# The first stage of a graph-attention kernel in another order: scores from PSUM, adj's first pair in two contiguous blocks masked on GpSimd, chunk steps between sides

## The reference

```python
h = maximum(layernorm(x), 0)                     # 4096 x 128
h = h @ W.T + b_W
e = (h @ a1)[:, None] + (h @ a2)[None, :] + b_a[0]
e = where(e > 0, e, 0.2 * e)                     # 4096 x 4096
scores = where(adj > 0, e, -9e15)
out = x + softmax(scores, axis=1) @ h
```

## Time and profile before

| | |
|---|---|
| median of 3 runs | 202.6 us (202.4 to 202.87) |
| span of the profiled execution | 200.8 us; its own time outside the span isn't recorded, the median is 1.8 us above it |
| TensorE busy | 194.9 us, 97% |
| VectorE | 183.0 us, 91% |
| ScalarE | 147.9 us, 74% |
| GpSimd | 52.4 us, 26% |
| DMA | 75.66 MB, 377 GB/s over the span |
| granted TensorE clock | 1.00 (2.4 GHz) throughout |

### The profile page before, as it was taken

How to read it: one execution, slowest core, us unless ns; L and a number is a source line. 1 busy time by engine, 2 the same in 40 slices (tenths; PEclk the granted TensorE clock), 3 DMA queues, 4 the chain that set the end, 5 groups by cost and what they waited for, 6 DMA issues and landing times.

```text
span 200.8 us, 7230 instructions
## 1 busy us (share of the span) xinstructions
PE 194.9 (97%) x3183; PEld 189.2 (94%) x3183; DVE 183.0 (91%) x265; ACT 147.9 (74%) x192; POOL 52.4 (26%) x66
## 2 busy tenths in 40 slices
PE   7969999999999999999999999999999999999993
PEld 7648889999999999999999999999999999999993
DVE  4779999999998799897999999999999999999745
ACT  2679879898882777689988888899588888996000
POOL 1002479699995010205000000072000000510000
PEclk9999999999999999999999999999999999999999
DMA  5999999999999999999999999999999999997012
GB/s 181 376 417 418 407 403 423 421 418 415 422 432 408 418 423 419 416 421 418 415 419 423 419 418 421 421 411 421 419 418 418 415 421 416 418 383 226 6 43 66
DMA packets 15968, 75.66 MB, mean 377 GB/s; under 512 B 1600, under 2 KB 5952, under 8 KB 7616
## 3 DMA queue, kind: packets, MB, share of 16 engines
q1 hardware_dynamic: 15792, 75.06, 91.7%
q10 hardware_dynamic: 144, 0.13, 0.3%
HBM read 73.08 MB, written 2.11 MB: 374 GB/s over the span
## 4 chain that ended last, share of the span: by engine, by line
PE 91%; DMA 4%; SPq 1%; DVE 1%; issue 1%; POOL 0%
PE ps L836 29%; PE ps L834 29%; PE ps L840 29%; DMA adj_sb<-in_adj_t 4%; PE ps L808 2%; PE ps L798 2%; SPq L268 1%; SPq L273 1%; PE ps L876 1%; DVE mask L476 0%; POOL bad L788 0%; DVE rden L504 0%; DVE rg L510 0%; DVE bad L519 0%; DVE upper L576 0%
## 5 line engine op out<-in xcount | busy, mean ns | idle before, releaser
L834 PE MATMUL ps<-V,w 128*128 128x129 f16 x1024 | 174.3, 221 | 0.0
L836 PE MATMUL ps<-V,w 128*128 128x129 f16 x1024 | 174.3, 221 | 0.0
L840 PE MATMUL ps<-V,w 128*128 128x129 f16 x1024 | 174.3, 221 | 0.0
L379 ACT ACTIVATE mask<-adj_sb 128x1024 bf16<-128x1024 int32 x126 | 125.5, 1056 | 28.6 <-DMA adj_sb<-in_adj_t 28.6
L459 DVE SCALAR_TENSOR_TENSOR w<-g_row,pairs,mask 128x1024 f32<-128x1024 f32 x96 | 120.5, 1320 | 5.5 <-ACT mask L379 3.6
L834 PEld LDWEIGHTS ps<-V,w 128*128 128x128 f16 x1024 | 100.2, 98 | 1.5 <-ACT H L340 0.7
L836 PEld LDWEIGHTS ps<-V,w 128*128 128x128 f16 x1024 | 100.2, 98 | 1.0 <-issue 1.0
L840 PEld LDWEIGHTS ps<-V,w 128*128 128x128 f16 x1024 | 100.2, 98 | 0.0
L459 DVE SCALAR_TENSOR_TENSOR w<-ps,pairs,mask 128x1024 f32<-128x1024 f32 x31 | 37.4, 1267 | 0.0
L785 POOL TENSOR_TENSOR xT<-xT,x_sb 128x512 f32<-128x512 f32 x6 | 11.5, 1932 | 79.8 <-ACT xT L394 79.8
L739 POOL TENSOR_TENSOR x_sb<-x_sb,b_row 128x512 f32<-128x512 f32 x8 | 10.0, 1301 | 0.0
(11 more groups left out here) (93 smaller groups left out, 63.8 us busy)
## 6 DMA issues: line engine op xcount, KB each, us to landing
adj_sb<-in_adj_t SPq DMA_DIRECT2D x64, 1024.0 KB, 10.3
xT<-in_x_t SPq DMA_DIRECT2D x8, 256.0 KB, 7.5
x_sb<-in_x_p SPq DMA_DIRECT2D x3, 512.0 KB, 10.9
g_row<-g_dram SPq DMA_DIRECT2D x1, 1536.0 KB, 10.3
out<-xT SPq DMA_DIRECT2D x3, 512.0 KB, 9.9
x_sb<-in_x_p SPq DMA_DIRECT2D x2, 256.0 KB, 4.2
out<-xT SPq DMA_DIRECT2D x1, 192.0 KB, 3.4
out<-xT SPq DMA_DIRECT2D x3, 64.0 KB, 1.6
```

Source lines behind the costliest of these rows:

```text
L379: nc.scalar.activation(mask[:, m % MASKS, r], adj_sb[:, m % HELD, r], ACT.Relu, scale=CONNECTED).then_inc(mask_ready, 1)
L834: nc.tensor.matmul(sums[:, bank, a, :], w16[:, m % SLOTS, col:col + P, 1], V[:, jt, 0, 0:NF], start=(jt == 0 and a == 0), stop=False, skip ...
L836: nc.tensor.matmul(sums[:, bank, a, :], w16[:, m % SLOTS, col:col + P, 1], V[:, jt, 1, 0:NF], start=False, stop=False, skip_group_check=True)
L840: last = nc.tensor.matmul(sums[:, bank, a, :], w16[:, m % SLOTS, col:col + P, 0], V[:, jt, 0, 0:NF], start=False, stop=(jt == NT - 1), ski ...
```

## The change

Scores of the first part are multiplied out of PSUM, by a new `first_scores` on VectorE as soon as the projections of chunks 0 and 1 are there; ScalarE copies these chunks to H only after that. The first pair of adj lies in DRAM as two contiguous blocks, one for each side, and is loaded by two transfers, the first of them ahead of x's chunks 2 and 3. Both of its masks are made by GpSimd. The low parts of chunk 0 and all of chunk 1 also go to GpSimd. The bias load is issued behind the load of m = 9. On TensorE `h_chunk(2)` comes behind the spread, the first pair's products with the low parts come last within its first side, and projection and centring steps stand between the sides of pairs 1 and 2. On ScalarE the masks of pairs 2 to 4 come later among the chunk steps. On GpSimd the deviations of the last sets come ahead of chunk 3's V.

```diff
-    H_BANK = (1, 4, 1, 4, 4, 4, 4, 4)
+    H_BANK = (1, 4, 4, 4, 4, 4, 4, 4)
+    V_AT = (1, 1, 2, 3, 4, 4, 5, 6, 7, 7, 8, 8, 9, 9)
...
@@ SP: loads
+                halves = adj_t[0, :, :].rearrange("p n -> (p n)").rearrange("(s p n) -> s p n", s=2, p=P)
                 load_xt(0)
+                load_x(0)
                 load_xt(1)
-                load_x(0)
                 load_x(1)
+                sp.dma_start(adj_sb[:, 0, 0:GC], halves[0, :, :]).then_inc(adj_begun, 16)
                 load_xt(2)
+                load_xt(3)
+                sp.dma_start(adj_sb[:, 0, GC:2 * GC], halves[1, :, :]).then_inc(adj_loaded[0], 16)
                 load_x(2)
-                load_xt(3)
-                load_adj(0)
+                load_adj(1)
                 load_xt(4)
-                load_adj(1)
...
                     load_adj(m)
+                    if m == BIAS_AT:
+                        sp.dma_start(b_row[:], b_W.rearrange("(a n) -> a n", a=1).to_broadcast([P, DOUT])
+                                     ).then_inc(b_row_loaded, 16)
@@ ACT
                 def take_chunk(c):
                     act.wait_ge(h_done, c + 1)
+                    if c < 2:
+                        act.wait_ge(scores_ready, 1)
...
                 roots_part()
+                nc.scalar.activation(warm[:], zero_col[:], ACT.Exp)
                 take_chunk(0)
+                weights(0)
                 take_chunk(1)
-                nc.scalar.activation(warm[:], zero_col[:], ACT.Exp)
                 relu_chunk(2)
-                weights(0)
+                highs(0)
                 relu_chunk(3)
-                highs(0)
-                first_mask()
                 take_chunk(2)
                 mask_part(1)
                 take_chunk(3)
                 relu_chunk(4)
-                highs(1)
-                mask_part(2)
                 take_chunk(4)
                 relu_chunk(5)
+                mask_part(2)
+                take_chunk(5)
+                relu_chunk(6)
                 weights(1)
                 mask_part(3)
-                take_chunk(5)
-                relu_chunk(6)
-                mask_part(4)
                 take_chunk(6)
                 relu_chunk(7)
+                mask_part(4)
+                take_chunk(7)
                 mask_part(5)
-                take_chunk(7)
@@ DVE
+                def first_scores():
+                    dve.wait_ge(h_done, 2)
+                    dve.wait_ge(std_ready, 2)
+                    for c in range(2):
+                        r = slice(c * CT, (c + 1) * CT)
+                        of = ps[:, H_BANK[c]:H_BANK[c] + 2, 0:2 * (2 + DOUT)].rearrange("p k (a n) -> p k a n", a=2)
+                        by = rstd[:, 1, r].rearrange("p (k a n) -> p k a n", k=2, n=1).to_broadcast([P, 2, 2, 2])
+                        ins = nc.vector.tensor_tensor(st[:, r, :].rearrange("p (k a) n -> p k a n", k=2),
+                                                      of[:, :, :, 0:2], by, ALU.mult)
+                    ins.then_inc(scores_ready, 1)
...
+                (statistics(1), norm, 1/std, first_scores, maximum of the scores,)
                 (then the three instructions on cc and the two on gg, then the read-back and the shifts)
-                early_mask()
+                step_(nc.vector.tensor_scalar(rstd[:, 2, 0:GI], rstd[:, 1, 0:GI], gg[:, 1:2], None, ALU.mult))
+                inverse_scales(0)
                 pack(0)
                 scale_weights(0)
-                products(0)
                 weigh_first(0)
-                lows(0)
                 weigh_first(1)
                 weigh(0, 1)
-                statistics(2, 5, 8)
+                statistics(2)
                 weigh(1, 0)
                 weigh(1, 1)
-                products(1)
-                lows(1)
+                statistics(3)
+                weigh(2, 0)
                 scores(1)
-                weigh(2, 0)
                 weigh(2, 1)
                 pack(1)
                 scale_weights(1)
-                statistics(3)
                 weigh(3, 0)
+                statistics(4)
                 weigh(3, 1)
-                statistics(4)
@@ GpSimd
+                def first_mask(side):
+                    if side == 0:
+                        pool.wait_ge(adj_begun, 16)
+                    else:
+                        pool.wait_ge(adj_loaded[0], 16)
+                    r = slice(side * GC, (side + 1) * GC)
+                    nc.gpsimd.tensor_scalar(mask[:, 0, r], adj_sb[:, 0, r], CONNECTED, 0.0, ALU.mult,
+                                            ALU.max).then_inc(mask_early if side == 0 else mask_first, 1)
+                first_mask(0)
+                first_mask(1)
+                first_lows()
+                halves(1)
                 deviations(2, 3)
-                halves(2)
+                halves(2, 0, 2)
+                halves(2, 2, 4)
+                deviations(3, 5)
                 halves(3)
-                deviations(3, 5)
@@ PE
+                centre_chunk(0), wa, norm, centre_chunk(1), h_chunk(0), h_chunk(1), cc
                 (transpose of the maxima, centre_chunk(2), centre_chunk(3), spread)
+                h_chunk(2)
+                first_pair()
                 h_chunk(3)
                 centre_chunk(4)
-                whole(0)
+                side_products(1, 0, 0, GI)
                 h_chunk(4)
                 centre_chunk(5)
-                whole(1)
+                side_products(1, 1, 0, GI).then_inc(mm_done, 1)
                 h_chunk(5)
                 centre_chunk(6)
-                whole(2)
+                side_products(2, 0, 0, GI)
                 h_chunk(6)
                 centre_chunk(7)
-                whole(3)
+                side_products(2, 1, 0, GI).then_inc(mm_done, 1)
                 h_chunk(7)
-                for m in range(4, NM - ENDS):
+                for m in range(3, NM - ENDS):
```

157 lines of the change are left out of this document (77 added, 80 removed).

## The result

The change makes the kernel slower: 208.27 us median (207.81 to 210.54) against 202.5 in the runs beside it, a ratio of 1.0296 with a 95% interval of 1.0238 to 1.0354. The profiled execution has a span of 206.7 us where the kernel before had 200.8. The forecast was 203.2, range 201.7 to 204.3: wrong in size by 5 us and outside its range.

The account below looks back on a forecast made before the run. TensorE's fixed sequence of attention products was taken as the bound. To 202.6 us were added 0 for the start, 0.45 for chunk 3's late V and 0.2 for the eighth pair: 203.2, range 201.7 to 204.3 (own range 202.4 to 204.5).

Parts of the forecast that it names:

- What bounds the kernel: TensorE's attention products are fixed work, 2.72 us a pair; only the sequence's start and holes in it change the time.
- Part 1, the chain to the pack: Projections, scores, maximum and exponentials before the first pack: pack ready at 11.55, 1.8 us earlier if nothing stands in its way.
- Part 2, the mask's price: First pair's masks on GpSimd: 1.2 us each, range 0.95 to 2.1, the second lying from about 11.5 to 12.7.
- Part 3, what the mask does to the pack: GpSimd's second mask holds VectorE's first pack until it ends: spread at 13.37, 1.0 of the 1.8 us lost.
- Rival (a): First pack on VectorE not held by the second mask: faster, 202.05 us, or 201.5 without the later hole; chance 0.28.
- Part 4, behind the spread: Chunk 2's projection, 0.89 us, now behind the spread, cancels the 0.79 gained: put at 0, no hole for low parts.
- Part 5: Sides, chunk steps, work taken from VectorE and the moved bias load: 0.
- Parts 6 and 7: TensorE waits 0.45 us at the seventh pair for chunk 3's V from GpSimd, then 0.2 for the eighth pair's weighting.
- rival (c): Holes at the seventh and eighth pairs don't open, since GpSimd starts chunk 3's V earlier: 202.5 us; chance 0.12.
- (b): Mask on GpSimd takes 2.5 us or more: 204.5 us, or 206.5 at 3.5 us a mask; slower, chance 0.10.

Follow-up runs that it names:

- e9_fewer_fillers: Changed kernel with 34 calls of float32 products that nobody reads, put on TensorE ahead of its wait for the first low parts; 214.43 us.
- e12_changed_again: The changed kernel once more, unaltered, on the same chip as a run with 17 filler calls; 209.42 us.
- e4_price: Kernel before, with six mask-like instructions of various types and sizes on GpSimd ahead of its deviations, results unused; 218.25 us, a time that means nothing.
- e7_masks_on_vector: Changed kernel with both first-pair masks on VectorE and ScalarE's order for the second pair as before; 202.52 us, 1.0003 of the kernel before.
- e10_v3_first: Changed kernel with chunk 3's V put back ahead of the last sets' deviations on GpSimd; 210.95 us.

## Why the prediction was wrong, step by step

- *What bounds the kernel*: right. The sequence of products is fixed work, and the loss is a late point of it plus holes in it; behind the eighth pair nothing changes.
- *Part 1, the chain to the pack*: the order was right, its start was not. The scores are done at 10.11 and the maximum is read back at 11.00, not 9.4 and 10.25; the pack starts at 12.26, 1.09 earlier than before and not 1.8. The term that failed is the end of the projections, 9.83 and not 9.05: the first two centring products, from 4.79 to 6.50, go at half the pace of the next two (0.86). The tables print a granted clock of 1.00 there, but the trace has no record of the clock before 6.51, and the pace tells the level: in every trace products go at half the pace until the records begin and at the full one from there, as between the levels of 1.2 and 2.4 GHz. In e9_fewer_fillers the warm-up products are 0.21 us apart up to its first record at 4.12 and 0.11 behind it; the two centring products take 0.87 there. In the kernel before the full pace begins at 4.83, in the other runs between 4.12 and 10.22, whatever the order. So the walk was right for a full pace from the start (in e9_fewer_fillers the projections end at 8.65 and the pack begins at 11.10), and when the pace rises is a term that the forecast didn't have. The 0.8 us for the five moved small instructions was right (10.22 to 11.00).
- *Part 2, the mask's price*: this is the step that failed. "It is nearer to the fill, and I take 1.2, with 0.95 to 2.1 for the range": it takes 3.645. Neither row was of such an instruction; a fill reads nothing, and a two-input multiplication, taken for the upper bound because it reads more, is the faster of the two. The halves landed at 8.26 and 10.84, 0.7 earlier than reckoned, which gave nothing, since GpSimd didn't start before 10.16. That start is a second miss in the same step: the trace of the kernel before has fills from 0.5 us on and arithmetic from 18.8 on, so no row showed when arithmetic can begin. No run divides the hole between the two. By the rows, masks of 1.2 us would have been through at 12.6 even from 10.16 on, and masks of 3.6 us begun at the landing would have ended at 15.6, 1.9 earlier than they did: as an estimate the price is enough for nearly the whole hole, and the start is worth up to half of it.
- *Part 3, what the mask does to the pack*: failed as well, since the hold has another length than the mask. VectorE's timeline of the kernel after, first and third pack, then GpSimd's masks and one instruction of VectorE in e9_fewer_fillers and in e12_changed_again:

```profile
12.26 0.18 DVE L583 TENSOR_SCALAR bounded<-eg 128x16 f32<-128x16 f32 x1 [0.24 <-ACT eg L367]
12.47 0.17 DVE L586 TENSOR_SCALAR upper<-bounded 128x16 int32<-128x16 int32 x1
12.68 0.18 DVE L589 CAST pairs<-upper 128x16 f16<-128x16 f32 x1
...
13.93 1.41 DVE L472 SCALAR_TENSOR_TENSOR w<-ps,pairs,mask 128x512 f32<-128x512 f32 x2 [0.93 <-POOL mask L763]
...
45.78 0.61 DVE L586 TENSOR_SCALAR upper<-bounded 128x32 int32<-128x32 int32 x1
46.43 0.55 DVE L589 CAST pairs<-upper 128x32 f16<-128x32 f32 x1
```

```profile
11.21 7.28 POOL L763 TENSOR_SCALAR mask<-adj_sb 128x1024 bf16<-128x1024 int32 x2 [9.78 <-DVE H L567]
11.31 0.98 DVE L586 TENSOR_SCALAR upper<-bounded 128x16 int32<-128x16 int32 x1
```

```profile
11.18 7.28 POOL L763 TENSOR_SCALAR mask<-adj_sb 128x1024 bf16<-128x1024 int32 x2 [9.75 <-issue]
11.58 0.68 DVE L639 TENSOR_SCALAR rstd<-rstd,gg 128x8 f32<-128x8 f32 x1
```

  In the profile of the change the first pack runs at its full pace in the middle of a 3.6 us mask that began 2.1 us before it; the third, beside a multiplication on GpSimd, is held to that instruction's end as in the earlier trace rows. But a mask does hold VectorE at its beginning. In the seven other traces with the first mask on GpSimd one tensor-by-constant instruction of VectorE takes 0.42 to 0.98 us instead of about 0.2, and each time it ends 1.06 to 1.08 us behind the mask's start (11.21 + 1.08 = 12.29 and 11.18 + 1.08 = 12.26 above), while the mask goes on for 2.6 us more; in e4_price it is 1.27 (the 0.59 at 14.87). In the profile of the change no instruction of this kind with more than one column began in that stretch, 10.16 to 11.24. The forecast had the second mask meet the pack, begun at 11.48 against 11.55; if the second mask holds as the first does, which no run shows, the pack's first instruction would have ended at 12.56 instead of 12.73, whatever the mask's price. In this run it was the first mask that lay beside the pack, and it had begun early enough. The rule of the Trainium skill that the prediction weighed (SBUF — State Buffer, Who interferes with whom), that the first to issue keeps the ports for its whole instruction, agrees with the third pack and not with the masks. Rival (a)'s condition, a pack that isn't held, was met in this run; its gain did not follow.
- *Part 4, behind the spread*: "net 0" is right, as e7_masks_on_vector shows by itself: spread 0.93 earlier, pair 4 at the same time. That the spread (13.08, in the range given of 13.0 to 13.7) and the first product (14.87 against 15.2) came out near the forecast is luck: the late scores took 0.7 of the 1.0 us that the hold of the pack was to take. "No hole" is wrong. The low parts were walked to 15.9 from free factors; that GpSimd must first be through with both masks entered the sum only as 1.2 us ending at 12.7. They came at 19.68. The prediction asked what the mask delays on VectorE, and not enough what is queued behind it on its own engine.
- *Part 5*: 0, right: from the spread to pair 4 e7_masks_on_vector takes 34.35 - 13.23 = 21.12 us, the kernel before 34.33 - 14.16 = 20.17, and of the 0.95 between them chunk 2's projection is 0.89; from pair 1 to pair 4 the changed kernel takes 14.56 and e7_masks_on_vector 14.53.
- *Parts 6 and 7*: right in mechanism and size: 0.54 and 0.14 against 0.45 and 0.2. The releasers are those named (GpSimd's subtraction for chunk 3), and in e10_v3_first the hole is gone with the deviations behind V. But they are one of two causes: e7_masks_on_vector keeps them ahead of V and has no such hole either. There ScalarE makes the second part's exponentials earlier, so GpSimd begins chunk 2's V 5.5 us behind pair 1 (25.33 - 19.82) and not 8.4 (33.37 - 25.00). That is rival (c)'s condition, brought about by another order. A slip of addition, 39.6 for 39.7 in TensorE's walk, makes the forecast of this hole 0.1 too long; another, 201.5 for 201.6 in rival (a), changes nothing.
- *The rivals*: (b) had the true engine, price and sign, with 0.10 and the sentence "No row speaks for such a price". For 3.5 us it gave 206.5. It let the masks start at 9.0 and so end at 16.0 instead of 17.44, took the late thing to be the pack, where it was the low parts two instructions further down GpSimd's queue, and left out the clock, 1.64.

The sum, forecast against measured: parts 1 to 4, 0 against a rest of -0.1 without the masks' queue; the hole, 0 against 3.7; the clock, 0 against 1.6, a term that the forecast didn't name; parts 6 and 7, 0.65 against 0.68. Together 0.6 against 5.9.

## What to carry to other kernels

Where an operation moves to an engine on which the trace has no such row, the nearest rows are not bounds: leave the upper end open, and ask first what stands behind it in that engine's queue and who waits for that. A hole on TensorE costs more than its length if the clock falls in it: count the pace behind it as a term of its own. Before a difference in the first microseconds of two profiles is put down to the change, the pace of TensorE's products there has to be compared. And an earlier start of a sequence gains only what it takes out of idle time; work that lay in the wait and is moved behind it takes the gain back.

## What the runs showed of the hardware that I had not expected

- GpSimd's tensor-by-constant instruction: 3.62 to 4.02 us for 1024 columns with two operations, in integers or floats (3.3 ns a column between 512 and 1024), 2.78 us with one; VectorE needs 0.69 us.
- Such an instruction on GpSimd holds a tensor-by-constant instruction of VectorE (8 or 16 columns) until 1.06 to 1.08 us behind its own start (seven traces; 1.27 in e4_price) and not for the 2.6 us that it still has to run; a two-input one holds it to its end (0.61 beside 0.62).
- GpSimd's first arithmetic in a run doesn't start before 10.16 to 11.42 us (once 14.19), whatever it is, while its fills run from 0.5 us.
- In the four traces with a stretch of 3.7 us without work on TensorE the granted clock falls to 0.50, in the first until 23.6 us, in e12_changed_again until 25.0; with products in the stretch it stays 1.00. Price: 1.6 to 2.0 us behind the hole. One execution of the changed kernel has a mean of 0.999, so there it hardly fell; how long its hole was isn't known.
- At the start of a run TensorE's products go at half the pace until 4.12 to 10.22 us, and the records of the granted clock begin only there.
- 68 products more in TensorE's program made its last branch 3.4 to 3.9 us long, 34 left it at 0.36. Which of the two applies decided the time of an experiment, so the stretch in question has to be read, not only the total.
